# One transformer layer on one core: the second layer norm folded into weights and thresholds, x1 turned by way of memory

## The reference

```
x1 = x + Attn(layernorm(x))            # Q, K, V with D = 64; energy = K^T V per batch
                                       # Attn = (Q @ energy) * sqrt(3/64) @ wo^T
h  = square(relu(layernorm(x1) @ W_fc^T))      # 1024 hidden columns
y  = h @ W_proj^T                              # back to 256
out = x1 + spikes(y) / 5
```

## Time and profile before

| | us |
|---|---|
| median of the runs | 482.85 |
| the profiled execution | 483.47 |
| its span | 481.7 |
| TensorE busy in the span | 466.1 |
| VectorE, ScalarE, GpSimd busy | 364.7, 285.5, 236.8 |

### The profile page before, as it was taken

The page is one execution under the profiler, slowest core; times in us unless marked ns, Lnnn a source line. Parts: engine busy times, 40 slices in busy tenths (PEclk is TensorE's granted clock), DMA queues, the critical chain, the costliest instruction groups (busy, mean ns, idle before and its releaser), DMA issues.

```text
span 481.7 us, 8498 instructions
## 1 busy us (share of the span) xinstructions
PE 466.1 (97%) x3004; PEld 420.1 (87%) x3004; DVE 364.7 (76%) x982; ACT 285.5 (59%) x519; POOL 236.8 (49%) x196
## 2 busy tenths in 40 slices
PE   7699899999999999999999999999999999999995
PEld 6588698998999989898998989899989989999995
DVE  4767758887878879787879878787888875939447
ACT  4518665756575665756666575666657565656540
POOL 1724556373655447374554637355453734445440
PEclk9999999999999999999999999999999999999999
DMA  8513021050503204050311305041210101010102
GB/s 283 142 46 74 15 44 46 11 122 2 131 2 75 57 37 97 1 132 0 82 51 55 79 1 132 1 91 42 59 30 1 45 1 46 0 45 1 46 12 77
DMA packets 60714, 26.63 MB, mean 55 GB/s; under 512 B 55552, under 2 KB 56192, under 8 KB 60416
## 3 DMA queue, kind: packets, MB, share of 16 engines
q1 hardware_dynamic: 60672, 26.09, 20.6%
HBM read 17.69 MB, written 8.39 MB: 54 GB/s over the span
## 4 chain that ended last, share of the span: by engine, by line
PE 89%; DVE 7%; DMA 1%; issue 1%; ACT 1%; SPq 0%; POOL 0%; DVEq 0%; ACTq 0%
PE y_ps L817 12%; PE y_ps L816 12%; PE y_ps L815 12%; PE hid_ps L815 12%; PE hid_ps L816 12%; PE hid_ps L817 12%; PE work_ps L857 3%; PE work_ps L926 1%; PE work_ps L925 1%; DVE cnt L716 1%; PE work_ps L893 1%; PE kv_ps L815 1%; DMA xs<-x_dram 1%; PE kv_ps L816 1%; PE kv_ps L817 1%; PE e_ps L906 1%
## 5 line engine op out<-in xcount | busy, mean ns | idle before, releaser
L341 POOL TENSOR_TENSOR hid_l<-hid,hid_h 128x512 fp32r<-128x512 f32 x128 | 165.2, 1295 | 211.8 <-ACT hid_h L395 211.6
L384 ACT ACTIVATE relu<-hid_ps 128x512 f32<-128x512 f32 x128 | 76.6, 598 | 113.0 <-PE hid_ps L817 112.6
L817 PE MATMUL y_ps<-wdn_h,hid_l 128*128 128x256 f32 x480 | 135.7, 283 | 0.0
L816 PE MATMUL y_ps<-wdn_l,hid_h 128*128 128x256 f32 x480 | 135.6, 283 | 0.0
L815 PE MATMUL y_ps<-wdn_h,hid_h 128*128 128x256 f32 x480 | 135.1, 282 | 0.0
L815 PE MATMUL hid_ps<-x2T_h,wup_h 128*128 128x512 f32 x256 | 105.4, 412 | 0.4 <-DVE x2T_l L634 0.4
L816 PE MATMUL hid_ps<-x2T_l,wup_h 128*128 128x512 f32 x256 | 100.7, 393 | 0.0
L817 PE MATMUL hid_ps<-x2T_h,wup_l 128*128 128x512 f32 x256 | 100.1, 391 | 0.0
L815 PEld LDWEIGHTS y_ps<-wdn_h,hid_h 128*128 128x128 f32 x480 | 91.4, 190 | 5.1
L816 PEld LDWEIGHTS y_ps<-wdn_l,hid_h 128*128 128x128 f32 x480 | 91.5, 191 | 4.9
L817 PEld LDWEIGHTS y_ps<-wdn_h,hid_l 128*128 128x128 f32 x480 | 91.4, 191 | 0.0
(11 more groups left out here) (127 smaller groups left out, 612.3 us busy)
## 6 DMA issues: line engine op xcount, KB each, us to landing
xs<-x_dram SPq DMA_DIRECT2D x15, 512.0 KB, 4.1
out_dram<-x SPq DMA_DIRECT2D x15, 512.0 KB, 2.9
x_block<-x_dram SPq DMA_DIRECT2D x104, 64.0 KB, 2.7
hid<-w_up_dram SPq DMA_DIRECT2D x1, 1024.0 KB, 8.1
x<-w_down_dram SPq DMA_DIRECT2D x1, 1024.0 KB, 10.2
xs<-x_dram SPq DMA_DIRECT2D x2, 256.0 KB, 3.4
out_dram<-x SPq DMA_DIRECT2D x1, 256.0 KB, 2.0
out_dram<-x SPq DMA_DIRECT2D x2, 128.0 KB, 1.9
```

Of the source, the lines that this page charges most:

```text
L341: nc.gpsimd.tensor_tensor(hid_l[:, i % 2, c, :], hid[:, c % 4, :], hid_h[:, i % 2, c, :].bitcast(f32), ALU.subtract).then_inc(hid_ready, 1)
L384: nc.scalar.activation(relu[:, c % 2, :], hid_ps[c % 2][:, :], ACT.Relu).then_inc(relu_done, 1)
L816: mm(dst, a[0], b[1], start=False, stop=False)
L817: return mm(dst, a[1], b[0], start=False, stop=stop)
```

## The change

1. **The norm is folded.** `w_up` is centred (its mean over the 256 inputs taken away: `average_up` on TensorE, `centre_up` on VectorE), as wkv and wq already are, so that x1 itself can be projected. The scale is squared by the square of the relu, and so goes to the other side of the comparison: the five thresholds are multiplied per token by (variance + eps) (`bound`), and the spikes compare with those. `normalise`, the inverse deviation on GpSimd and x2n go.
2. **x1 is turned by way of memory.** For groups 2 to 15, SyncE writes x1 to a DRAM tensor `x1_blocks` in four DMAs of 128 KB in runs of 128 bytes (`scatter_x1`), waits, and reads it back in one DMA with 4 KB a partition (`gather_x1`) into x_block, where VectorE turns it (`turn_x1`). Groups 0 and 1 are turned by TensorE. x_block and the tile `turned` serve x and x1 in turn.
3. **GpSimd** takes the low half of the turned x1 (two instructions of 128x512, at c = 7, ahead of `low_half(7)`) and that of kv (one, at c = 6), from VectorE.
4. **Moved:** on TensorE `energy_sum` from c = 1 to 0, `energy_times_wo` from 2 to 1, `attend` from 3 to 2, `project_kv` from 6 to 4, `turn_kv` from 7 to 5, with ScalarE's and VectorE's parts of them; on VectorE `residual` ahead of `first_moments`; in the start most of the filler transposes (`keep_warm`) go or give way to `average_up`.

```diff
+            def scatter_x1(n):
+                sp.wait_ge(x1_ready, n + 1)
+                if n >= 4:
+                    sp.wait_ge(x1_blocks_back, 16 * (n - 3))
+                for b in range(4):
+                    src = x1[32 * b:32 * (b + 1), n % RING, :].rearrange("q (s i e) -> q s i e", s=TILES * EC, i=4)
+                    sp.dma_start(x1_blocks[n % 2, :, :, :, b, :].rearrange("i q s e -> q s i e"), src)\
+                        .then_inc(x1_blocks_written, 16)
+            def gather_x1(n):
+                sp.wait_ge(x1_blocks_written, 64 * (n - 1))
+                sp.wait_ge(x_turn, min(n, GROUPS - BY_MATMUL))
+                sp.dma_start(x_block[:, :], x1_blocks[n % 2].rearrange("i q s b e -> (i q) (s b e)"))\
+                    .then_inc(x1_blocks_back, 16)
             def step(r, i):                                  # SyncE
-                if there(r, i + RING) and not (isinstance(r, int) and i < 0):
-                    load_blocks(r, i + RING)
+                if there(r, i - 2):
+                    store(r, i - 2)
+                if there(r, i + 1) and not x1_by_matmul(i + 1):
+                    scatter_x1(i + 1)
+                    gather_x1(i + 1)
                 if there(r, i + RING + 1):
                     load(r, i + RING + 1)
-                if there(r, i - 1):
-                    store(r, i - 1)
+                if there(r, i + RING) and i >= 0:
+                    load_blocks(i + RING)                    # now waits for turn_x1(i + 1) too
...
+            def x2T_low_half(n):                             # GpSimd
+                for k in range(EC):
+                    pool.wait_ge(x2T_high, EC * n + k + 1)
+                    low, high = (half[:, n % 2, k, :].rearrange("p (t n) -> p t n", t=TILES) for half in (x2T_l, x2T_h))
+                    last = nc.gpsimd.tensor_tensor(low, x1_turned(n, k), high.bitcast(f32), ALU.subtract)
+                last.then_inc(x2T_ready, 1)
...
+                    if c == 6 and there(r, i + 3) and not is_first(r, i):
+                        kv_low_half(r, i + 3)
+                    if c == 7 and there(r, i + 1) and not x1_by_matmul(i + 1):
+                        x2T_low_half(i + 1)
                     if c == 2 and there(r, i + 3) and not is_first(r, i):
                         x_low_half(r, i + 3)
                     if there(r, i):
                         low_half(r, i, c)
...
+                    if c == 4 and there(r, i + 3):           # ScalarE, after square(c)
+                        kvT_out(r, i + 3)
                     if c == 6 and there(r, i + 3):
-                        kvT_out(r, i + 3)
+                        kv_high_half(r, i + 3)
                     if c == 6 and there(r, i + 1):
                         x2T_high_half(r, i + 1)
...
+            def turn_x1(n):                                  # VectorE
+                dve.wait_ge(x1_blocks_back, 16 * (n - 1))
+                dve.wait_ge(xT_ready, min(n + 3, GROUPS))
+                if n >= GROUPS - 2:
+                    dve.wait_ge(x2T_ready, n)
+                nc.vector.transpose(turned[:, :], x_block[:, :]).then_inc(x1_turn, 1)
...
+                    nc.vector.scalar_tensor_tensor(
+                        bound[:, n % RING, :, :], mv[b][:, :, 1:2].broadcast_to([P, TILES, NUM_STEPS]), EPS,
+                        theta[:, :].unsqueeze(1).broadcast_to([P, TILES, NUM_STEPS]), ALU.add, ALU.mult).then_inc(bound_ready, 1)
...
-                        nc.vector.scalar_tensor_tensor(acc, y, THETA[level], acc, ALU.is_gt, ALU.add)\
+                        nc.vector.scalar_tensor_tensor(acc, y, limit(level), acc, ALU.is_gt, ALU.add)\
...
+                if there(r, i + 3):                          # VectorE's step, middle of pair 0
+                    kv_scale(r, i + 3)
+                if there(r, i + 1) and not x1_by_matmul(i + 1):
+                    turn_x1(i + 1)
                 if there(r, i - 1):
                     spikes(r, i - 1, 0, range(PAIR_OPS // 2, PAIR_OPS))
...
+            def average_up(h):                               # TensorE
+                pe.wait_ge(w_loaded["up"], 16)
+                pe.wait_ge(xT_ready, 2)
+                rows = wup_raw.rearrange("p (k n) -> p k n", k=EC)
+                for k in range(EC):
+                    last = mm(hid_ps[h][:, :], averager[:, :], rows[:, k, h * HID // 2:(h + 1) * HID // 2],
+                              start=(k == 0), stop=(k == EC - 1))
+                last.then_inc(wup_mean, 1)
```

More of the change, by code:

```diff
@@ L292, in _ @@
             load(0, 3)
-            load_blocks(0, 3)
-            for i in range(-1, GROUPS):
+            load_blocks(3)
+            for i in range(-1, GROUPS + 1):
                 step(0, i)
@@ L308, in _ @@
             nc.gpsimd.memset(neg_half[:, :], -0.5).then_inc(half_ready, 1)
+            for level in range(NUM_STEPS):
+                nc.gpsimd.memset(theta[:, level:level + 1], THETA[level]).then_inc(theta_ready, 1)
             pool.wait_ge(ident_zero, 1)
@@ L387, in square @@
                 act.wait_ge(relu_done, upto(r, i, FC, c + 1))
+                if i == 0 and c == 1:
+                    act.wait_ge(wup_ready, 2)
                 if there(r, i - 1) or c > 3:
@@ L500, in step @@
                     high_half(r, i, FC - 1)
-                if there(r, i + 3):
-                    kv_high_half(r, i + 3)
             high_half_of_weights(wkv_centred, wkv_raw[:, :], wkv_h, wkv_high)
@@ L566, in kv_low_half, with centre_up, moments @@
                 nc.vector.tensor_tensor(low, src, as_f32(high), ALU.subtract).then_inc(kv_ready, 1)
[L568 to L578 removed]
+            def centre_up(h, k):
+                dve.wait_ge(wup_mean, h + 1)
+                rows = wup_raw.rearrange("p (k n) -> p k n", k=EC)[:, k, h * HID // 2:(h + 1) * HID // 2]
+                nc.vector.tensor_tensor(rows, rows, hid_ps[h][:, :], ALU.subtract).then_inc(wup_centred, 1)
+            def moments(n, which):
+                if which:
+                    b = 2
+                    if n:
+                        dve.wait_ge(bound_ready, n)
+                else:
+                    b = n % 2
+                    if n >= 2:
+                        dve.wait_ge(rstd_ready, n - 1)
                 for t in range(TILES):
[L580 removed]
+                    if t == TILES // 2 and n == 0 and which == 0:
                         dve.wait_ge(x_loaded[0], 16)
@@ L633, in x2T_low_half, with turn_blocks @@
                     dve.wait_ge(x2T_high, upto(r, n, EC, k + 1))
-                    last = nc.vector.tensor_tensor(x2T_l[:, n % 2, k, :], turn2_banks(r, n)[k][:, :],
-                                                   as_f32(x2T_h[:, n % 2, k, :]), ALU.subtract)
+                    low, high = (half[:, n % 2, k, :].rearrange("p (t n) -> p t n", t=TILES) for half in (x2T_l, x2T_h))
+                    last = nc.vector.tensor_tensor(low, x1_turned(n, k), as_f32(high), ALU.subtract)
                 last.then_inc(x2T_ready, 1)
-            def turn_blocks(r, n):
-                dve.wait_ge(x_block_loaded, counted(r, BLOCK_LOADS * (n - BY_MATMUL + 1), BLOCK_LOADS * UNROLL))
-                dve.wait_ge(x2n_turned, upto(r, n - 2))
-                nc.vector.transpose(x2n[:, :], x_block[:, :]).then_inc(x_turn, 1)
+            def turn_blocks(n):
+                dve.wait_ge(x_block_loaded, BLOCK_LOADS * (n - BY_MATMUL + 1))
+                if n > BY_MATMUL:
+                    dve.wait_ge(xT_ready, n)
+                if n >= 5:
+                    dve.wait_ge(x2T_ready, n - 2)
+                nc.vector.transpose(turned[:, :], x_block[:, :]).then_inc(x_turn, 1)
             def q_low_half(r, n):
@@ L676, in spikes, with limit @@
             def spikes(r, n, pair, ops):
+                def limit(level):
+                    return bound[:, n % RING, 2 * pair + a, level:level + 1]
                 for o in ops:
@@ L761, in step @@
                     eo_low_half(r, i + 2)
+                if there(r, i + 1):
+                    residual(r, i + 1)
                 if there(r, i + 3):
                     first_moments(r, i + 3)
-                if there(r, i + 1):
-                    residual(r, i + 1)
-                    moments(r, i + 1, 1)
+                if there(r, i):
+                    moments(i, 1)
                 if is_last(r, i - 1):
@@ L987, in first_step @@
                         turn_kv(0, 2)
+                        turn_x1(1)
                     if c == 6:
@@ L1039, in _ @@
             project_kv(0, 1)
+            average_up(0)
             project_q(0, 1)
@@ L1045, in _ @@
             energy_times_wo(0, PER_BATCH - 1)
-            keep_warm(2)
+            average_up(1)
             attend(0, 0)
-            keep_warm(12)
-            turn_second(0, 0)
-            keep_warm(4, work_ps[1])
+            keep_warm(4)
+            turn_x1(0)
+            keep_warm(3, work_ps[1])
             steps(pe, step)
```

203 lines of the change are left out of this document (104 added, 99 removed).

## The result

The changed kernel takes 553.79 us (median of five, 550.44 to 554.77) against 484.08 us for the kernel before in the same runs (482.57 to 484.79): a ratio of 1.1432, 95% interval 1.1407 to 1.1457. The forecast was 548 in a range of 510 to 582. The profiled execution took 550.44 us, with a span of 548.7, 67.0 more than before.

A forecast was written before the change was run, and what follows sets the result against it. TensorE's sum plus the start bounds the kernel: 483.5 - 12.2 (transposes) - 6.2 (start) + 60.5 (waits) = 525.6 us, plus 23.8 for the clock = 549, rounded to 548; range 510 to 582.

The forecast's parts named there:

- The wait: End of steps 1 to 14: TensorE stands still for GpSimd's x1 low half, 12 x 4.4 + 2 x 3.85 = 60.5 us.
- the ring TensorE, ScalarE, GpSimd: Inside each step, `project_up(7)`, `rectify(7)`, `high_half(6)`, `low_half(6)` and x1's low halves hold up TensorE; nothing takes the wait back.
- ScalarE's: At c = 6 a longer ScalarE row makes `rectify(7)` begin at about U + 2.2, 0.55 us late.
- U: The start of `project_up(7)` at a step's end; TensorE was forecast to go on at U + 7.3, not U + 2.89.
- GpSimd's part: From `rectify(7)` on: 1.19 us to `low_half(6)`, its 1.27, two x1 low halves 2.56, wake-up 0.05; together 5.07 us.
- The clock: Falls to half behind each standstill, in the next step's c = 0: 1.7 us in 14 steps, 23.8 us.
- Rival 1: At the step ends the wait comes, but the clock stays up: 525.6 us; chance 0.21.
- The trip through memory: From the end of `residual` to the turned x1: 11.7 us (9.2 to 13.1) inside 12.2; cost taken as 0.
- Rival 2: Stores in 128-byte runs land at half rate, so `turn_x1` is 3.5 us late in 14 steps: 597 us; chance 0.12.
- The start: -2.7 us before the first `project_up`, -3.5 in step 0; together -6.2, between -2 and -8.
- The thresholds: In the spike comparisons, thresholds from a tile instead of a constant: nothing, 0.2 us a pair would still be hidden.
- Rival 3: Faster than before if the step-end standstill is below 1.3 us a step; 465 us with no wait; chance 0.09.

The follow-up runs named there:

- the doubled store: Changed kernel with every part of x1 written a second time, to another DRAM tensor, the read waiting for both: 585.0 us, ratio 1.2115.
- the version in time: Changed kernel with x1's low half back on VectorE right behind `turn_x1`, and ScalarE's high half right behind `rectify(6)`: 486.7 us, ratio 1.0054.
- that of the start: The version in time with group 0's `moments` behind a kv low half, and group 1's kv high half ahead of `high_half_of_up(0)`: 482.1 us, ratio 0.9961.
- the 474 us version: That of the start with q, energy, `energy_times_wo`, its conversions and group 3's inverse deviation moved in the engines' orders: 474.03 us, ratio 0.9795.
- GpSimd's order: Changed kernel with GpSimd's low half of the turned x1 ahead of `low_half(6)` instead of behind it: 524.63 us, ratio 1.0845.
- VectorE instead of GpSimd: Changed kernel with the low half of the turned x1 given back to VectorE, at the end of its step: 523.31 us, ratio 1.0825.
- the version in time without the trip: The version in time without scatter and gather, x_block turned as it lies (x1 values wrong for groups 2 to 15): 480.45 us, ratio 0.9918.

## Why the prediction was right

- *The wait.* The place, the releaser and the number of waits are as forecast: 14, behind the ring TensorE, ScalarE, GpSimd. The size was 3.83 us, not 4.4 (53.3 us, not 60.5). The term that was most too large is ScalarE's: `rectify(7)` began at U + 1.86, 0.2 us late and not 0.55, since ScalarE begins an instruction 0.52 us after the one before and not after its full 0.62. GpSimd's part, forecast at 5.07 from `rectify(7)` on, took 252.71 - 247.77 = 4.94. In the last two steps the wait was 3.57 and 3.70, forecast 3.85. Moving the x1 pair one place forward takes off 1.4 us a step; it then stands behind GpSimd's low half of kv, which the prediction did not reckon with and which the changed kernel hides.
- *The clock.* It fell behind thirteen of the fourteen waits. Forecast 23.8 us; 23.9 in windows, 20 to 21 by filling the gap. The prediction has the whole fall behind the standstill. But eight of the thirteen begin before TensorE resumes, and 2.3 of the 23.9 us lie there and cost nothing; 21.6 are left. The profiled execution was the fastest of five, with a mean granted clock of 0.948; the other four have 0.934 to 0.940 and took 3.0 to 4.3 us longer. In the run with constants as thresholds a fall goes with all fourteen waits. Rival 1 is out. The Trainium skill (TensorE: Matmul & The Clock Gate, HAM oscillation) has the cold clock paid again after each wait; by that rule, the trace agrees in thirteen steps of fourteen.
- *The steps.* From the `project_up(0)` of step 2, at 89.86, to that of step 15, at 506.69, lie 13 steps, 32.06 us each. In the kernel before they take from 85.75 to 441.64, 27.38 each. The difference is 4.69: 3.81 of waiting, 0.87 less for the turn, and 1.75 left for the clock (21.6 / 13 = 1.66 by the windows). These are the three terms of the forecast.
- *The trip through memory.* Forecast 11.7 us from the end of `residual`, with a room of 0.5; it was 10.45 with 1.6. The four issues took 2.77 and not 4.1, because a store of 1024 runs of 128 bytes is issued in 0.69 us, about as fast as a load of 512 such runs (5.35 / 8 = 0.67). The load back took 3.6 and not 4.1, and 0.8 were spent behind `kv_scale`, which the sum did not have. Rival 2 is out as the cause, though the doubled store showed that it was 1.6 us away.
- *The start: wrong.* Forecast -6.2 us, of which -2.7 ahead of the first `project_up` and -3.5 in step 0. The first `project_up` began at 36.88 and not before 35.85. Step 0 did gain: the `project_up(0)` of step 1 began at 55.99, where it had begun at 57.73, so that step 0 was 2.8 us shorter. Step 1 lost it again: without its wait, the `project_up(0)` of step 2 would have begun at 89.86 - 3.83 = 86.03, against 85.75 before. With the 0.87 that the turn in step 1 no longer costs, the start has lost 1.2 us, and the forecast was 7.4 off: 3.7 ahead of the first `project_up`, 0.7 in step 0, 2.9 in step 1. The terms missed are two. GpSimd's subtraction on w_up, now at 20.95 instead of 15.44, fell beside VectorE's kv low half:

```profile
23.89 1.12 PE L1002 MATMUL e_ps<-kv 128*128 128x128 f32 x4 [4.81 <-DVE kv L637]
...
21.42 2.42 DVE L637 TENSOR_TENSOR kv<-kv_scaled,kv 128x512 fp32r<-128x512 f32 x1 [1.64 <-ACT kv L470]
```

Such waits were 1.5 and 2.1 us long in the kernel before. The clock lay at half for about 6.8 us around it, where it had been about 3.4 before. And `energy_sum` in c = 0 of step 1 found VectorE 2.44 us late. Undoing the first gave most of 4.6 us: the first `project_up` of that version began at 33.02, 2.8 before the 35.85, while in the other traces of the changed start it lies between 35.8 and 37.5. So -2.7 could be had, but not in the order that the change has.
- *The thresholds: a miss of up to two microseconds.* 0.06 us each, hidden in the steps as said, but not at the end, which the forecast left as before. The last 20 comparisons end the kernel: 11.8 us from the first of them to the end of the last result, 10.6 before and 10.6 with constants. The eight ahead of them take 3.2 us, and 2.7 with constants.
- *Rival 3.* Its point (a wait under 1.3 us) is borne out in part. With the standstill gone, the version in time was still 0.5% above the kernel before; with the start mended it was 0.4% below, and with the last moves 2%. Its full 465 was not reached. The spans differ by 9.1 us from it, and the 474 us version shows where. The `project_up(0)` of its step 2 begins at 80.01, where the forecast's start would have it at 85.75 - 0.87 - 6.2 = 78.7: 1.3 us. Its 13 steps from there take 26.96 us each and not 27.38 - 0.87 = 26.51: 5.9 us. Its end takes 41.9 us and not 40.1: 1.8 us.

```profile
80.01 0.40 PE L902 MATMUL hid_ps<-x2T_h,wup_h 128*128 128x512 f32 x1
```

In sum: 483.5 - 12.2 + 53.3 + 21.6 for the clock, 1.2 for the start and 1.9 for the end (40.06 us behind the last `project_up(0)` before, 42.01 after) give 549.3, and 550.4 was measured in the profiled execution. The prediction's own sum is 549.4, which it rounds to 548. That it came so close is partly luck: the waits were put 7.2 us too high, the clock 2.2, and the start 7.4 and the end 1.9 too low.

## What to carry to other kernels

When a step of the next stage's input is given to another engine, don't ask whether that engine has time, but what stands ahead of the step in its order and what that waits for: here an engine that was busy for half of the time (49% before, 50% after) held up one at 97%. Count a standstill of the matmul engine together with the slower clock behind it, and where one can't be avoided, fill it. A VectorE instruction with two SBUF operands and a GpSimd instruction that reads SBUF should be given different moments.

## What was not expected of the hardware

- A standstill of 2.33 to 2.49 us was enough for the clock to fall in ten of twelve steps of two versions, and one of 1.95 us once, while the last one of 3.70 us in the changed kernel had no fall behind it. TensorE's waits in the steps of the 474 us version, up to 1.3 us, had none either. One wait in step 1, 2.40 to 2.44 us long, stands in nine of the traces: the clock fell behind it in five (GpSimd's order, VectorE instead of GpSimd, the doubled store, the version in time and that of the start) and not in four (the changed kernel, the filler, the constants, and the version in time without the trip). The length of the standstill alone does not decide, and what does was not tested.
- Filler transposes in the standstill kept the clock up and gave 21 us back. They cost little: over eleven steps one takes 31.01 us with them, and the changed kernel's 32.49 less 1.69 for its falls is 30.8.
- VectorE and GpSimd reading SBUF together: 1.29 us became 2.35, 0.75 became 2.32, and 2.53 became 3.35.
- A threshold per partition instead of a constant: 471 against 408 ns for 128x256 read from PSUM.
- Stores to DRAM in runs of 128 bytes: a median of 0.68 us of issue and 2.7 us to landing for 128 KB, where a load of 64 KB in such runs takes 0.64 and 2.6. They keep up with the loads, but a store of 512 KB with 4 KB a partition lands in 2.6 us as well.
